# Moving the making of V from the gaps of the offset chain into eight units of the taps

## What is computed

```python
x = x + attention(group_norm(x))          # 8 heads of 48 over the 1024 pixels, then w_proj, b_proj
x = x + deform(group_norm(x))

def deform(x):
    offset = clip(conv3x3(x, off_w, off_b), -8, 8)       # 18 channels
    mask = 2 * sigmoid(conv3x3(x, mask_w, mask_b))       # 9 channels
    y = sum over 9 taps of proj_w[tap] @ bilinear_sample(x, position(tap) + offset[tap]) * mask[tap]
    return gelu(batch_norm(y + proj_b) * gamma + beta)   # statistics over all 8 images
```

## Time and profile before

| | us |
|---|---|
| median of 3 runs (lowest to highest) | 3851.82 (3846.78 to 3856.44) |
| the profiled execution | 3852.39 |
| its span, first to last instruction | 3850.4 |
| PE busy | 3482.5 |
| DVE busy | 2304.3 |
| ACT busy | 1628.6 |
| POOL busy | 1274.1 |

### The profile page before, as it was taken

One profiled execution on the slowest core, in us unless ns is written; L12 is line 12 of the kernel. 1 busy time (PEld: TensorE's weight loads), 2 busy tenths in 40 slices (PEclk: granted clock), 3 DMA queues, 4 the chain that ended last, 5 costly groups with the idle time before them and its releaser, 6 DMA issues.

```text
span 3850.4 us, 88793 instructions
## 1 busy us (share of the span) xinstructions
PE 3482.5 (90%) x33434; PEld 1879.6 (49%) x33434; DVE 2304.3 (60%) x3746; ACT 1628.6 (42%) x2644; POOL 1274.1 (33%) x1182
## 2 busy tenths in 40 slices
PE   5798999989999899998999899998999989998991
PEld 2244554645445455454545454454544545454661
DVE  5585565755657566665666556575565756665343
ACT  3064333733336433453335433373333643344443
POOL 0062232712326223342325233271232612343440
PEclk8689999999999999999999999999999999999996
DMA  3000000000000000000000000000000000001007
GB/s 127 0 19 34 1 1 36 3 34 1 1 36 2 34 1 1 36 35 1 1 2 36 34 1 1 17 21 34 1 1 36 2 34 1 1 19 67 1 2 295
DMA packets 12152, 97.80 MB, mean 25 GB/s; under 512 B 2778, under 2 KB 2906, under 8 KB 4973
## 3 DMA queue, kind: packets, MB, share of 16 engines
q1 hardware_dynamic: 9468, 67.41, 4.5%
q0 software_dynamic: 1152, 12.58, 0.8%
q10 hardware_dynamic: 1008, 11.01, 0.7%
HBM read 56.26 MB, written 34.60 MB: 24 GB/s over the span
## 4 chain that ended last, share of the span: by engine, by line
PE 55%; issue 22%; POOL 14%; ACT 4%; DVE 3%; DMA 1%; POOLq 0%; DVEq 0%; SPq 0%; ACTq 0%
PE R L1492 20%; PE R L1473 14%; POOL PL L607 13%; PE G L1270 7%; PE G L1237 5%; PE G L1461 2%; PE R L1385 2%; PE R L1310 1%; ACT PL L830 1%; PE G L1453 1%; PE G L1412 1%; PE G L1407 1%; ACT P L769 1%; DMA QK<-x_scratch 1%; DVE M L1166 0%
## 5 line engine op out<-in xcount | busy, mean ns | idle before, releaser
L1492 PE MATMUL R<-P,WALL 128*128 128x512 f16 x3888 | 984.8, 380 | 0.3 <-issue 0.3
L989 DVE TENSOR_REDUCE MXP<-G 128x1 f32<-128x512 f32 x1024 | 698.3, 689 | 258.4 <-PE G L1270 244.7
L607 POOL TENSOR_TENSOR PL<-P 128x1024 f16<-128x1024 f32 x256 | 573.8, 2246 | 635.1 <-ACT P L752 633.0
L1473 PE MATMUL R<-MHL,XB 128*128 128x240 f16 (+14 forms) x7776 | 726.5, 236 | 2.7 <-DVE P L1187 2.6
L644 POOL TENSOR_TENSOR MHL<-M,MHL 128x280 f16<-128x280 f32 (+2 forms) x576 | 364.6, 635 | 986.0 <-ACT MHL L840 984.7
L752 ACT ACTIVATE P<-R 128x1024 f32<-128x1024 f32 x512 | 520.8, 1023 | 239.7 <-PE R L1310 226.2
L1473 PEld LDWEIGHTS R<-MHL,XB 128*128 128x128 f16 x7776 | 536.4, 98 | 156.0 <-issue 110.3
L1039 DVE TENSOR_TENSOR PL<-P 128x1024 f16<-128x1024 f32 x256 | 453.3, 1771 | 177.4 <-ACT P L752 177.2
L1492 PEld LDWEIGHTS R<-P,WALL 128*128 128x128 f16 x3888 | 345.4, 98 | 416.4 <-issue 95.6
L1310 PE MATMUL R<-QK 48*128 48x512 f16 (+1 forms) x3072 | 437.8, 394 | 53.0 <-issue 31.7
L1270 PE MATMUL G<-QK 48*128 48x512 f16 x1024 | 412.7, 404 | 44.0 <-DVE QK L977 17.4
(11 more groups left out here) (125 smaller groups left out, 3240.3 us busy)
## 6 DMA issues: line engine op xcount, KB each, us to landing
XA<-x SPq DMA_DIRECT2D x8, 1536.0 KB, 9.0
X<-x SPq DMA_DIRECT2D x8, 1536.0 KB, 6.6
x_scratch<-X SPq DMA_DIRECT2D x7, 1536.0 KB, 5.1
y_scratch<-XP ACTq DMA_DIRECT2D x7, 1536.0 KB, 7.0
WALL<-y_scratch SPq DMA_DIRECT2D x6, 1536.0 KB, 15.3
out<-WALL POOLq DMA_DIRECT2D x6, 1536.0 KB, 10.9
QK<-x_scratch SPq DMA_DIRECT2D x4, 1536.0 KB, 17.1
P<-wd SPq DMA_DIRECT2D x9, 576.0 KB, 4.9
```

Of the source, the lines that this page charges most:

```text
L607: pool.tensor_tensor(PL[:, s % P_BUFS, :], P32[:, s % P_BUFS, :], high_view(s), ALU.subtract).then_inc(p_low_pool, 1)
L989: dve.reduce_max(MXP[:, name[1] % 2, n // 2, n % 2:n % 2 + 1], chunk(sec, name)[:, :], AX.X).then_inc(dve_read, 1)
L1473: last = pe.matmul(out, XT[:, x_part, g * BOX_Y + r, t * 128:(t + 1) * 128], MHL[:, m_part, o + at:o + at + (hi - lo) * (x1 - x0)], start= ...
L1492: last = pe.matmul(R6[:, CT + ct, :], WALL[:, w:w + 128], PHL[:, u % 2, part // 2, t, :], start=(u % TAPS == 0 and n < CT), stop=(u % TAPS ...
```

## The change

The eight V chunks leave the offset chain and the first hats. They become part of `CONV_FILL[6]` to `CONV_FILL[13]`, one each, ahead of the unit's maxima, so that they stand beside the convolutions of units 5 to 12. In units 7, 8, 9, 11, 12 and 13 V takes spot 6, and the four maxima move to spots 15, 18, 20 and 23; in units 6 and 10 `maxT` keeps spot 6, V takes 15, and the maxima 17, 19, 21 and 23. The reading of V by ACT and DVE moves with it. The programs of SP and POOL keep their text.

```diff
 DRAIN = QK[0:LAG + 1]
 GN_FILL = QK[LAG + 1:LAG + 3]
-POS_FILL = [("v", n) for n in range(6)]
-HX_FILL = [("v", 6), ("v", 7)]
+V_FILL = [("v", n) for n in range(QT)]
...
         convs[u] += made[:2]
         made = made[2:]
+        convs[u] += V_FILL[u - 6:u - 5] if u >= 6 and u < 14 else []
         count = 2 if u < 5 else 4
         convs[u] += maxima[:count]
...
-    fill = POS_FILL if start else [None] * len(POS_FILL)
-    out += [fill[0], ("comb",), fill[1], fill[2], ("pos", 0), ("mask", 0), fill[3], ("reach",), fill[4], ("pos", 1),
-            fill[5], ("mask", 1)]
-    return with_readers([n for n in out if n])
+    return with_readers(out + [("comb",), ("pos", 0), ("mask", 0), ("reach",), ("pos", 1), ("mask", 1)])
...
     out = [(("hx", 0, g), "A", 1) for g in range(BOX_X)]
-    out += with_readers(HX_FILL[:1] if start else [])
     out += [(("hy", 0, c), "D", weight(reach)) for c in range(ring(reach))]
-    out += with_readers(HX_FILL[1:] if start else [])
```

In the programs of ACT, DVE and PE every call that reads or fills a chunk of `POS_FILL` or `HX_FILL` is taken out, as here in PE's; nothing is put in their place, since the loops over `beside` take up the new names by themselves:

```diff
-                if not final:
-                    for name in POS_FILL[1:3]:
-                        fill_chunk(name, sec, b + 1)
                 hat_positions(sec, 0)
                 hat_masks(sec, 0)
-                if not final:
-                    fill_chunk(POS_FILL[3], sec, b + 1)
                 pe.wait_ge(rows_max, b + 1)
```

More of the change, by code:

```diff
@@ L799, in batch @@
                 for u in range(2):
-                    if not final:
-                        for name in (POS_FILL[1:3], POS_FILL[3:5])[u]:
-                            read_chunk(name, sec, b + 1)
                     name = ("pos", u)
                     hats(chunk(sec, name), u, sec.at(name, "A"))
-                if not final:
-                    read_chunk(POS_FILL[5], sec, b + 1)
                 act.wait_ge(reach_known, b + 1)
@@ L844, in taps @@
                         x_hats(0, g)
-                    if not final:
-                        read_chunk(HX_FILL[0], sec, b + 1)
                     for c in range(ring(reach)):
                         m_halves(0, c)
-                    if not final:
-                        read_chunk(HX_FILL[1], sec, b + 1)
                     for u in range(UNITS):
@@ L1083, in batch @@
                                           ALU.subtract).then_inc(xt_low, 1)
-                if not final:
-                    read_chunk(POS_FILL[0], sec, b + 1)
                 dve.tensor_scalar(CLIP, chunk(sec, ("comb",))[0:BOTH, :], CBIAS[0:BOTH, 0:1], -float(MAX_OFF),
@@ L1090, in batch @@
                 link(dve.tensor_scalar(CLIP, CLIP, float(MAX_OFF), IS_POS[0:BOTH, :], ALU.min, ALU.mult))
-                if not final:
-                    read_chunk(POS_FILL[1], sec, b + 1)
                 dve.wait_ge(act_read, sec.at(("comb",), "A"))
@@ L1108, in batch @@
                 position_halves(0)
-                if not final:
-                    read_chunk(POS_FILL[2], sec, b + 1)
                 dve.tensor_reduce(RMX[0:BOTH, :], CLIP, AX.X, ALU.max,
@@ L1118, in batch @@
                 dve.tensor_tensor(HL[:, 0, :], TV[:, cols_of(0)], H16, ALU.subtract).then_inc(first_hats, 1)
-                if not final:
-                    read_chunk(POS_FILL[3], sec, b + 1)
                 dve.reduce_max(FMX[:, 0:1], chunk(sec, ("reach",))[0:1, 0:128], AX.X).then_inc(dve_read, 1)
@@ L1124, in batch @@
                                   ALU.is_gt, ALU.add).then_inc(reach_known, 1)
-                if not final:
-                    for name in POS_FILL[4:6]:
-                        read_chunk(name, sec, b + 1)
                 dve.wait_ge(reach_known, b + 1)
@@ L1393, in batch @@
                         transposed(2)
-                if not final:
-                    fill_chunk(POS_FILL[0], sec, b + 1)
                 out = bank(sec, ("comb",))
@@ L1413, in hat_masks @@
                               start=True, stop=True).then_inc(chunk_full, 1)
-                if not final:
-                    for name in POS_FILL[1:3]:
-                        fill_chunk(name, sec, b + 1)
                 hat_positions(sec, 0)
                 hat_masks(sec, 0)
-                if not final:
-                    fill_chunk(POS_FILL[3], sec, b + 1)
                 pe.wait_ge(rows_max, b + 1)
                 pe.transpose(bank(sec, ("reach",))[0:1, 0:128], RMX[:, :], IDENT).then_inc(chunk_full, 1)
-                if not final:
-                    fill_chunk(POS_FILL[4], sec, b + 1)
                 hat_positions(sec, 1)
-                if not final:
-                    fill_chunk(POS_FILL[5], sec, b + 1)
                 pe.wait_ge(reach_known, b + 1)
@@ L1500, in taps @@
                         x_hats(0, g)
-                    if not final:
-                        fill_chunk(HX_FILL[0], sec, b + 1)
                     for c in range(ring(reach)):
                         y_hats(0, c)
-                    if not final:
-                        fill_chunk(HX_FILL[1], sec, b + 1)
                     for u in range(UNITS):
```

1 line of the change is left out of this document (removed).

## The result

The changed kernel takes 3886.44 us (median of 4 runs, 3883.55 to 3887.82) against 3849.32 us of the kernel before on the same chip (4 runs, 3846.78 to 3856.44). The ratio is 1.0092, 95% interval 1.0075 to 1.011: slower by 0.9%, well beyond the 0.3% that can be told from no change. The forecast was 3877 in a range of 3861 to 3896. The two profiled executions, 3883.55 and 3852.39 us, lie 31.2 apart; their spans, 3881.7 and 3850.4, differ by 31.3, and it is these 31.3 us that the rows can place. (The medians differ by 37, since the profiled run of after was the fastest of its runs and that of before lay above its median.)

What follows compares the result with a forecast made beforehand. PE was taken to bound the taps, and dependent DVE, ACT and PE steps the offset chain. Taps +11.8 less chain 8.2 gives +3.6 us a batch, +25 over seven on 3852.4: about 3877 us, range 3861 to 3896.

Steps and rivals of the forecast that it cites:

- The taps, added: Units 6 to 13: eight V chunks at 1.47 us each add 11.8 us a batch; lower bound 10.1.
- Rival 3: Packed taps: V's matmuls overlap beyond their columns, 1.03 us a chunk, sum zero, 3852 us; chance 2%.
- rival 4: Units 6 to 13: waits inside the samples set their ends, so V is hidden, 3795 us; chance 4%.
- The chain, saved: L785 copy to first tap convolution: without V 38.95 instead of 47.15 us, saving 8.2 a batch (5.2 to 10.6).
- The first term: Chain from the L785 copy to the hats of unit 1: 18.65 us, as batch 7 shows without V.
- The second term: Chain from the hats of unit 1 to the position matmul for unit 2: 5.71 us, batch 7's at low clock.
- The third: Position matmul for unit 2 to first tap convolution: 14.19 us as in batch 0, plus 0.4 for a second clock fall.
- rival 2: Chain: the clock falls twice, the second spell reaching unit 1; net 6.6 us a batch, 3898 us; chance 16%.
- Rival 1: Chain: the clock holds, saving 10.6 us, net +1.2 a batch, 3861 us; chance 8%.
- The bound of 36.56 us: Copy to first tap convolution with the clock at the upper level throughout: 18.65 + 3.72 + 14.19 us, a saving of 10.6.
- Reading V, costed at nothing: Units 6 to 13: ACT's 490 ns and DVE's 556 ns reads cost 0; uncovered, at worst 8.4 us a batch.
- The sum: Whole kernel: 11.8 - 8.2 = +3.6 us a batch, times seven batches +25 us.

Runs made afterwards that it cites:

- the mix: Against the kernel before: V chunks two between comb and first positions, one behind first y hats, two in units 6 and 7, three at batch end; 3835.26 us, ratio 0.9957.

## Why the prediction was right

**The bound.** PE sets the time in the taps, dependent steps set it in the chain: the run without V took 1.5 us a chunk out of units 6 to 13 and left the chain as it was (39.5 against 39.3).

**The taps, added.** Costed at 11.8 us a batch, measured 12.0. The chunk took 1.47 us in the units, as the row in the chain had said. Rival 3 (1.03 us a chunk) and rival 4 (V absorbed) fall with this number.

**The chain, saved.** Costed at 8.2, measured 7.8. The three terms, with the three windows of batch 0 in the changed kernel beside them:

```profile
353.71:372.75 19.04, 8.37 (x35) 3.05 (x35) 9.47 (x20) 6.10 (x13) 4.67 (x7) 0.68 0.00 1
372.75:378.26 5.51, 5.37 (x45) 4.68 (x45) 1.39 (x5) 1.67 (x4) 1.32 (x3) 0.57 0.00 0
378.26:393.50 15.24, 12.92 (x89) 7.68 (x88) 8.07 (x16) 6.82 (x14) 4.73 (x6) 0.89 0.01 1
```

To the hats of unit 1 19.04 to 19.28 us (a mean of 19.14) instead of 18.65, then a mean of 5.43 instead of 5.71, then 14.77 instead of 14.59. Batch 7 of the trace before was the right model in kind, its low clock included, but each term is off.

The first term has the largest miss, 0.5 us a batch. Some 0.36 of it stands ahead of the first position matmul, with the clock still at 1.00: it comes 5.85 to 5.97 us after the copy in batches 0 to 6 (359.56 - 353.71 in batch 0) and 5.50 in batch 7 (3552.71 - 3547.21 in the trace before). So batch 7's program, written out behind the loop, passes these first steps faster; why, no run shows. The second term was too large by 0.3, which hides part of this by luck. The third was mis-sized by 0.2: a second fall of the clock was taken to cost 0.4 us in the mean of seven batches, as in two of them before; it came in four of seven (15.24 to 15.36 us against 14.10), some 0.7. That is a piece of rival 2, which had the fall in every batch and at 3.4 us. Rival 1, a clock that holds, would have ended at 3861; the kernel with zero-weight matmuls shows what it would have taken for that, and ended at 3869. The bound of 36.56 us that it met was reached partly by luck: its 18.65 is batch 7's figure at a clock of 0.68, and the loop's slower first steps (0.36 more) and its higher clock behind them (0.42 less) happen to cancel to 18.6.

The Trainium skill, "TensorE: Matmul & The Clock Gate", section "HAM oscillation — how this bites in real kernels", has a TensorE that waits between bursts fall to half clock; all seven batches agree (0.53 to 0.65 from the hats of unit 1 to the position matmul of unit 2), with waits for other engines in place of the transfers that the page tells of.

**Reading V, costed at nothing.** Right for this change, and by less than the text gave it: it named about 2 us of matmuls as cover, but ACT's order leaves 0.44 us of margin, and the kernel with three matmuls a chunk lost 0.5 us there in each of six units.

**The sum.** +25 forecast, +31 in the profiled executions, +37 between medians. Some 1.4 of the 6 us between the first two is the taps' term (0.2 a batch), some 2.8 the chain's (0.4 a batch), the rest lies in neither stretch. All three miss in the same direction. One sum of the prediction is wrong by 2 us: the upper end of its range, 3896, is worked out as 3877 + 17, which is 3894; the measured time is below both.

Behind the prediction, two expectations were wrong in their reasoning. The end of the batch was taken for a wait that three chunks can fill, and they filled the 1.3 us of it that are ACT's copy of y. And the cheap places were expected to cost something, where the fuller PE gave back in clock what they took.

Open: whether the wait at the turn of the loop is the loading of PE's program, and why two pieces overlap there in some programs; what a fourth chunk at the end costs alone; and why the loop's first steps are slower than batch 7's.

## What to carry to other kernels

Work that fills gaps has one price in each place, and the place that looks wasteful can be the cheapest: ask of each chunk whether it stands in a wait (here free on balance), on the chain (1.87 us) or in a packed stretch (its columns, 1.5 us), and move only those that cost more than they would elsewhere. When gaps are emptied, the bare chain is not what comes back, because PE's clock fell behind the gaps that were left (0.74 to 0.82 in the chain against 0.89 to 1.00); a stretch of the same kernel that already runs without the fill, as batch 7 did, is the best model for it: the sum built on it was 0.4 us a batch short. And a wait without a releaser in the profile should not be counted as room until a run has put something into it.

## What was not expected of the hardware

The wait that the profile calls "issue", ahead of the first scores of the next batch, stands at each turn of the loop (6 times) and not where the program runs on behind it. It is not shortened by 4.4 us of work put ahead of it (6.41 us with V, 5.81 without, in the same place), and its length follows the program: 5.8 us at most in the changed kernel, 4.8 in the mix, 6.4 in the mix with more matmuls in the chain, 2.8 in the mix with a fourth chunk at the end. In each of these a 16 KB piece of the instruction queue lands 1.3 to 2.5 us before the scores. The wait can swallow a gain made elsewhere (6.7 us against 4.7).

Matmuls whose result nobody reads made the kernel 17.3 us faster: the granted clock in the chain rose (0.91 to 1.00, after 0.74 to 0.82), and the chain became 2.4 us shorter a batch, 16.5 in all.
